# State-space rounds of a decoder kernel: block sums by accumulated transposes, a third block convolved on TensorE, ScalarE's side work placed by half units

## The reference

```python
for i in range(4):                                   # x: 8 x 100 x 256
    h = rms(x, norm_w[i])
    xi, z = split(h @ W_in[i].T)                     # 512 channels each
    xc = silu(conv_b[i] + sum(shift(xi, 3-k) * conv_w[i][:, k] for k in range(4)))
    delta, Bm, Cm = split(xc @ W_x[i].T)             # 64, 16, 16
    delta = softplus(delta @ W_dt[i].T + b_dt[i])
    A = -exp(A_log[i])                               # 512 x 16 states
    deltaA, BX = exp(delta * A), (delta * xc) * Bm
    hs = scan(deltaA, BX)                            # h_t = deltaA_t h_{t-1} + BX_t
    y = sum_n(hs * Cm) + D[i] * xc                   # over the 16 states
    x = x + (y * silu(z)) @ W_out[i].T
```

## Time and profile before

| | |
|---|---|
| median of 3 runs | 1289.17 us (1286.73 to 1289.67) |
| the profiled execution | 1286.74 us, its span 1285.0 us |
| mean granted TensorE clock | 0.949 of 2.4 GHz |
| busy over the span | PE 88%, DVE 82%, ACT 64%, POOL 60% |
| state-space rounds | from 354 to about 1056 us |

### The profile page before, as it was taken

How to read it: one execution, slowest core, us unless ns; L and a number is a source line. 1 busy time by engine, 2 the same in 40 slices (tenths; PEclk the granted TensorE clock), 3 DMA queues, 4 the chain that set the end, 5 groups by cost and what they waited for, 6 DMA issues and landing times.

```text
span 1285.0 us, 17476 instructions
## 1 busy us (share of the span) xinstructions
PE 1128.5 (88%) x5960; PEld 660.0 (51%) x5960; DVE 1050.3 (82%) x1642; ACT 825.1 (64%) x1816; POOL 775.4 (60%) x641
## 2 busy tenths in 40 slices
PE   7798888879759998998998999989989689999974
PEld 3455555544325454554554545545545346666643
DVE  4577777675689999999999999999999985676657
ACT  1455555655466786777767767877776436788763
POOL 6001111100389898998998999989989952554202
PEclk9899999998979999999998999989999899999878
DMA  7000002000510600502404107014042003100000
GB/s 211 13 13 13 13 13 73 2 1 3 201 44 0 217 34 2 205 17 88 162 1 181 42 1 251 1 54 168 1 150 88 1 11 90 34 18 18 2 1 26
DMA packets 22141, 79.13 MB, mean 62 GB/s; under 512 B 4935, under 2 KB 8847, under 8 KB 21138
## 3 DMA queue, kind: packets, MB, share of 16 engines
q1 hardware_dynamic: 22054, 78.02, 17.7%
HBM read 76.77 MB, written 1.24 MB: 61 GB/s over the span
## 4 chain that ended last, share of the span: by engine, by line
PE 42%; DVE 33%; ACT 10%; POOL 8%; issue 7%; DMA 0%; DVEq 0%; SPq 0%; POOLq 0%; ACTq 0%
PE ps L675 38%; DVE ps L2089 10%; DVE arena L2094 6%; DVE arena L2092 5%; POOL arena L2003 4%; PE ps L744 4%; ACT ps L1886 2%; DVE hstat L1213 2%; POOL arena L2015 2%; DVE arena L2052 2%; ACT L670 1%; DVE arena L1189 1%; ACT arena L936 1%; DVE arena L1179 1%; ACT arena L1776 1%
## 5 line engine op out<-in xcount | busy, mean ns | idle before, releaser
L675 PE MATMUL ps<-arena 128*32 128x100 f32 (+10 forms) x3330 | 517.4, 380 | 67.3 <-ACT arena L936 14.6
L2003 POOL TENSOR_TENSOR arena<-arena 128x1600 f32<-128x1600 f32 x128 | 456.6, 3582 | 34.0 <-DVE ps L2089 25.8
L675 PE MATMUL ps<-arena,ident 128*128 128x400 f32 x1024 | 386.5, 528 | 29.4 <-POOL arena L2015 19.9
L675 PEld LDWEIGHTS ps<-arena 128*32 128x32 f32 (+7 forms) x3330 | 259.4, 144 | 294.3 <-issue 115.9
L1886 ACT ACTIVATE ps<-arena 128x400 f32<-128x400 f32 x512 | 282.9, 589 | 184.5 <-DVE arena L2092 151.3
L2089 DVE TENSOR_TENSOR_SCAN ps<-ps,arena 128x800 f32<-128x800 f32 x176 | 320.6, 1822 | 22.8 <-ACT ps L1886 17.1
L675 PEld LDWEIGHTS ps<-arena,ident 128*128 128x128 f32 x1024 | 201.5, 200 | 196.4 <-issue 28.3
L642 POOL TENSOR_SCALAR stat<-stat 100x1 f32<-100x1 f32 (+1 forms) x44 | 8.5, 193 | 419.9 <-DVE stat L623 419.0
L2092 DVE TENSOR_TENSOR arena<-ps,arena 128x800 f32<-128x800 f32 x176 | 174.5, 991 | 6.0
L2015 POOL TENSOR_TENSOR arena<-arena 128x1600 f32<-128x1600 f32 x40 | 143.1, 3579 | 16.8 <-DVE arena L2094 16.7
L2094 DVE TENSOR_TENSOR_SCAN arena<-ps,arena 128x800 f32<-128x800 f32 x80 | 140.3, 1803 | 0.9 <-ACT ps L1886 0.7
(11 more groups left out here) (199 smaller groups left out, 1025.7 us busy)
## 6 DMA issues: line engine op xcount, KB each, us to landing
arena<-bc_scratch SPq DMA_DIRECT2D x64, 800.0 KB, 6.4
arena<-in_ctxT SPq DMA_DIRECT2D x16, 361.0 KB, 4.0
arena<-in_w_in SPq DMA_DIRECT2D x4, 1024.0 KB, 5.0
arena<-in_expT SPq DMA_DIRECT2D x1, 2048.0 KB, 12.9
arena<-in_w_out SPq DMA_DIRECT2D x4, 512.0 KB, 3.2
arena<-in_mask SPq DMA_DIRECT2D x8, 141.0 KB
arena<-in_xT SPq DMA_DIRECT2D x2, 400.0 KB, 4.1
x_tok<-in_x_tok SPq DMA_DIRECT2D x1, 800.0 KB
```

The source lines that it names most:

```text
L675: return nc.tensor.matmul(outp, lhsT, rhs, start=first, stop=last)
L2003: nc.gpsimd.tensor_tensor(bx[:, unit % BX].rearrange("p (j t) -> p j t", j=SEGMENT), bbc[:, nq].rearrange("p (j t) -> p j t", j=SEGMENT), ...
```

## The change

1. Sums by transposes (`pm_reduce`): for blocks 0 to 2 the four identity matmuls of a unit become 16 transposes of 100 columns each, accumulated in the same bank: the sum over states comes out turned (100 tokens on partitions, 4 x 128 columns). A one-row product first starts the bank. ScalarE copies a block's turned sums to SBUF (`am_turned_sums`), TensorE turns them back onto diag(D) times xc in the same bank (`pm_back`), and VectorE's y product waits for that. Block 3 is summed as before.
2. Block 1 is convolved on TensorE too: taps for three blocks, one more `pm_conv`, and on ScalarE a raw copy and an output for it; VectorE keeps block 0, three multiply-adds, one chain.
3. ScalarE's and VectorE's lists go by half units (`am_half`, `am_between`), and nearly every place in `AT` is new. The copies `am_keep` have a place of their own. On POOL the step rows of blocks 2 and 3 stand at 19 and 21 and not at 16 and 17.

```diff
-    "aK": 2,
-    "aQ": 4,
+    "aQ": 3.0,
+    "aV": 3.5,
...
-    "aV": 3,
-    "aS": 11,
...
+    "aS": 10.5,
...
-    "aD": (13, 14),
+    "aD": (13.0, 14.5),
...
-    "gD": (14, 15, 16, 17),
-    "vY": (5, 10, 13, 16),
+    "gD": (14, 15, 19, 21),
+    "aYT": (6.0, 10.0, 13.5),
+    "pY": (6, 10, 14),
+    "vY": (6.0, 10.5, 14.5, 16.5),
...
         def pm_reduce(pe, unit):
...
+            if c < CD - 1:
+                if nq == 0:
+                    mm(ps[0:S, 4 + c % 2, :], identb[0:1, 1:S + 1],
+                       identb[0:1, :].rearrange("p (o t) -> p o t", o=1).to_broadcast([1, GB, P]), True, False)
+                for j in range(SEGMENT):
+                    for b in range(GB):
+                        last = nc.tensor.matmul(ps[0:S, 4 + c % 2, b * P:(b + 1) * P],
+                                                hs[:, unit % HS, j * GT + b * S:j * GT + (b + 1) * S], ident[:, :],
+                                                is_transpose=True, start=False,
+                                                stop=nq == NQ - 1 and j == SEGMENT - 1 and b == GB - 1)
+                last.then_inc(m_red, 1)
+                return
...
+        def pm_back(pe, m, c):
+
+            pe.wait_ge(m_yt, (CD - 1) * m + c + 1)
+            pe.wait_ge(m_skip, m // G + 1)
+            o = ps[:, 4 + c % 2, 0:GT]
+            mm(o, dgd[:, c], xc[m % G][:, c], True, False)
+            for b in range(GB):
+                last = nc.tensor.matmul(o[:, b * S:(b + 1) * S], turned_rows(c)[0:S, b * P:(b + 1) * P], ident[0:S, 0:S],
+                                        is_transpose=True, start=False, stop=b == GB - 1)
+            last.then_inc(m_yb, 1)
...
+        def am_turned_sums(act, m, c):
+
+            act.wait_ge(m_red, UNITS * m + NQ * (c + 1))
+            nc.scalar.activation(turned_rows(c)[0:S, :], ps[0:S, 4 + c % 2, :], ACT.Copy).then_inc(m_yt, 1)
...
         def vm_y(dve, m, c):
...
-            dve.wait_ge(m_red, UNITS * m + NQ * (c + 1))
+            if c < CD - 1:
+                dve.wait_ge(m_yb, (CD - 1) * m + c + 1)
+            else:
+                dve.wait_ge(m_red, UNITS * m + NQ * CD)
```

More of the change, by code:

```diff
@@ L297, in decoder @@
         delta[1] = mam.take(CD, GT)
-        taps = mam.take(2, DC, P)
-        mam.at += CD * GT - 2 * DC * P
+        taps = mam.take(3, DC, P)
+        mam.at += CD * GT - 3 * DC * P
         dx = mam.take(CD, GT)
@@ L1396, in decoder @@
         m_taps = sem("m_taps")
+        m_yt, m_yb = sem("m_yt"), sem("m_yb")
         ROUNDS = G * NL
-        PREP = (["T0", "T1", "X2", "X3", "Y2", "Y3", "X0", "X1", "DB"] + [f"D{c}" for c in range(CD)]
+        PREP = (["T0", "T1", "X2", "X3", "Y2", "Y3", "X1", "X0", "Y1", "DB"] + [f"D{c}" for c in range(CD)]
                 + [f"X{e}" for e in range(CD, 2 * CD)])
@@ L1570, in pm_conv @@
             for s in range(DC):
-                last = mm(y3[:, :, s:S], taps[:, c - 2, DC - 1 - s], x3[:, :, 0:S - s], s == 0, s == DC - 1)
+                last = mm(y3[:, :, s:S], taps[:, c - 1, DC - 1 - s], x3[:, :, 0:S - s], s == 0, s == DC - 1)
             last.then_inc(m_full, 1)
@@ L1701, in mam_pe @@
                             pm_dbc(pe, m + 1)
-                        for c in range(CD):
+                        for c in (0, 1):
                             if u == AT["pD"][c]:
@@ L1831, in am_silu @@
                 return
[L1832 removed]
+            for names, c in ((("Y2", "Y3"), 2), (("X0", "Y1"), 0)):
                 for n in names:
@@ L1866, in am_skip, with am_half @@
             last.then_inc(m_skip, 1)
-        def am_unit(act, unit):
+        def am_half(act, k):
+            unit, h = divmod(k, 2)
             m, u = divmod(unit, UNITS)
@@ L1872, in am_unit @@
             l, g = divmod(m, G)
-            if nq == 0:
+            if nq == 0 and h == 0:
                 act.wait_ge(m_first, CD * m + c + 1)
@@ L1876, in am_unit @@
                     act.wait_ge(m_aneg, l + 1)
-            for h in range(2):
-                k = 2 * unit + h
-                if unit:
-                    if on_dve(unit - 1):
-                        act.wait_ge(m_cmd, dve_halves(unit - 1, h))
-                    else:
-                        act.wait_ge(m_scan, k - 1)
-                for j in range(2):
-                    n = c * NS + nq * SEGMENT + 2 * h + j
-                    last = nc.scalar.activation(psf[:, half_at(k) + j * GT:half_at(k) + (j + 1) * GT],
-                                                delta[g][:, c], ACT.Exp, scale=aneg[:, l % 2, n:n + 1])
-                last.then_inc(m_exp, 1)
+            if k >= 2:
+                before, bh = divmod(k - 2, 2)
+                if on_dve(before):
+                    act.wait_ge(m_cmd, dve_halves(before, bh))
+                else:
+                    act.wait_ge(m_scan, k - 1)
+            for j in range(2):
+                n = c * NS + nq * SEGMENT + 2 * h + j
+                last = nc.scalar.activation(psf[:, half_at(k) + j * GT:half_at(k) + (j + 1) * GT],
+                                            delta[g][:, c], ACT.Exp, scale=aneg[:, l % 2, n:n + 1])
+            last.then_inc(m_exp, 1)
         def mam_act(act):
@@ L2094, in vm_half @@
                 nc.vector.tensor_tensor_scan(y, a, bx[:, unit % BX, w], 0.0, ALU.mult, ALU.add).then_inc(m_scan, 1)
-        def vm_unit(dve, unit):
-            wait(dve, m_red, unit - HS + 1)
-            dve.wait_ge(m_bx, unit + 1)
-            for h in range(2):
-                vm_half(dve, unit, h)
         def vm_y(dve, m, c):
```

229 lines of the change are left out of this document (128 added, 101 removed).

## The result

| | before | after |
|---|---|---|
| median of the runs of one comparison | 1287.95 us (1282.80 to 1289.67, 4 runs) | 1320.06 us (1317.96 to 1322.64, 4 runs) |
| the profiled execution, its span | 1286.74, 1285.0 us | 1317.96, 1316.2 us |
| mean granted TensorE clock | 0.949 | 0.913 |

The ratio on record is 1.0271 with a 95% interval of [1.0249, 1.0293] (it is an estimate of its own; the quotient of the two medians is 1.0249): slower, as forecast (1310 us), 10 us beyond the forecast's centre.

The account below looks back on a forecast made before the run. VectorE's queue plus waits bounds a round: 84.15 - 1.5 + (1.7 + 2.4 + 1.1 + 1.4) + 0.2 + 0.9 = 90.35 us against 87.05. Six rounds +20, the first +1: 1310 us, range 1300 to 1320.

Parts of the forecast that it names:

- before 3.5: Second half of unit 3: exponentials queue behind the output rows' squares, the third waiting for output sum O1; 1.7 us a round.
- before 4.0: First half of unit 4: the gate's silu with two table loads, 4.14 us, delays the exponentials; 2.4 us a round.
- before 11.0: First half of unit 11: the convolved blocks' silu, moved to 10.5, delays the exponentials; 1.1 us a round.
- before 13.5: Second half of unit 13: first softplus, 3.69 us, moved to 13.0 where room is 2.3; wait 1.4 us a round.
- the room of two halves less two pairs: Time a ScalarE step may last between exponentials without VectorE waiting: 3.3 us between long halves, 2.3 beside one short, 1.3 between short.
- T: End of half 9.5, the second half of unit 9, from which ScalarE's steps up to exponentials 11.0 were timed.
- The transposes: TensorE's sums: 0.086 us each, 1.4 us a unit for 2.7, saving 16 us a round; cover, valued at 0.6 us.
- The clock: TensorE at 1.2 GHz after idling 22 to 31 us into the round and near 60 to 75; 0.9 us, bounds 0 to 3.2.
- Rival 2: PE stays at 1.2 GHz through the transposing blocks, making y products and reductions late: 3.2 us a round, 1325 us; chance 0.16.
- Rival 1: ScalarE enters the new places a half ahead, so only 2.3 us of wait at 4.0 is left: 1276 us; chance 0.15.
- Rival 3: Transposes run at a matmul's rate, so PE sets the round at about 95 us: 1340 us; chance 0.04.
- Rival 4: The orders cancel: two of the four waits fall away, a round of 87 us, no change; chance 0.07.

Follow-up runs that it names:

- the fourth: The changed kernel with blocks 0 and 1 both convolved on VectorE again, six steps, transposes kept: 1321.02 us, 1.0293 against the kernel before.
- the fifth experiment: The changed kernel with sums by identity matmuls and blocks 0 and 1 convolved on VectorE, only the new order left: 1322.46 us, 1.0296 against the kernel before.
- the third experiment: The changed kernel with all sums by identity matmuls again, places and block 1's convolution on TensorE kept: 1304.96 us, 1.0151 against the kernel before.
- the filled kernel: The changed kernel with nine unused 128x400 matmuls a round behind the sum of unit 3, where TensorE stood idle: 1311.34 us, 1.0210 against the kernel before.
- The first of the three kernels with other places: The changed kernel's work, transposes and third block included, with places chosen by the rule of rooms: 1271.36 us, 0.9914 against the kernel before.
- the last three kernels: Places by the rule of rooms, with transposes and third block, matmuls and third block, or the work of before: 1271.36, 1267.27, 1275.38 us.

## Why the prediction was right, point by point

| wait of VectorE, us a round | forecast | after |
|---|---|---|
| before 3.5 (third square behind O1) | 1.7 | 1.82 |
| before 4.0 (silu of z behind it) | 2.4 | 2.52 |
| before 11.0 (silu of the convolved blocks) | 1.1 | 1.63 |
| before 13.5 (softplus) | 1.4 | 1.54 |
| low clock: y product of block 0, sum of unit 15 | 0.9 | 1.92, all of it block 0 |
| what else (forecast at 15.0; found at the y product of block 3) | 0.2 | 0.27 |
| VectorE's queue without waits | 82.65 | 82.4 |
| a round | 90.35 | 92.1 |

*The bound.* Right: VectorE's queue and its waits set the round, and the room of two halves less two pairs gave all four places and, at 3.5, 4.0 and 13.5, the size within 0.15 us. The same chain, put into the kernel before, gave the same two waits.

*The convolution.* The term was right, 1.5 us off VectorE's work, but beside the transposes it bought nothing. The experiment that puts it back shows that the waits around it shrink by the same 1.5. With sums by matmuls and the same places it did take 1.5 us off a round (92.4 to 90.9).

*The wait at 11.0*, 1.63 for 1.1, and the 1.1 was partly luck: two steps of it failed, in opposite directions. The first is "Exponentials 10.0 end at T - 0.65": it leaves out the convolution between the halves 9.0 and 9.5, which by the prediction's own rule adds its 1.9 us to the room. They end at 772.22, 2.3 before T, the start of the scan 10.0. The second is "the copy of the turned sums and the result of block 1 at T + 0.55": I let the copy run at once, but it waits for TensorE:

```profile
771.11 1.11 ACT L1933 ACTIVATE ps<-arena 128x400 f32<-128x400 f32 x2 [0.61 <-DVE arena L2154]
774.56 1.80 DVE L2149 TENSOR_TENSOR_SCAN ps<-ps,arena 128x800 f32<-128x800 f32 x1
774.67 0.60 ACT L1866 ACTIVATE arena<-ps 100x512 f32<-100x512 f32 x1 [2.45 <-PE ps L1617]
```

The last sum of block 1 is ready that late. With only the first step mended, copy and result would have been done before T, exponentials 10.5 would have ended at T + 1.1, those of 11.0 at T + 6.55, and the wait would have been 0.5. That is near the 0.66 of the fourth and the fifth experiment, which convolve block 1 on VectorE. Without the copy but with the result of block 1, in the third experiment, it was still 1.2 to 1.3: there the result waits 2.61 us for TensorE.

*The transposes*, mis-sized: 0.086 us, taken from eight of 100 columns with 100 rows, against 0.11 for these at the full clock, 1.8 us a unit for 1.4. The step that failed is taking a time for 100 moving columns as one for 128: 0.086 x 1.28 is the 0.11 found. A transpose of 128 columns costs half of a matmul's 0.21 for as many. It sets no bound, since PE is busy 78.5 of 92 us, but I had expected about 70: PE gained 2 to 3.5 us and not 11. At 0.11 the twelve units save 10.8 us and not 16, and in the early stretch of low clock the work takes longer. Against the third experiment, which differs from after in the sums alone, PE is busy 5.7 us less in a round (78.6 for 84.25).

*The clock*, mis-sized: 0.9, a value chosen inside the bounds 0 to 3.2, against 1.92. The first idle place was right, 22 to 31 us into the round forecast and 24.4 to 30.7 found. The second came later than forecast: the clock is at 0.50 from 74 to 81 us into the round, for "near 60 to 75", and the 1.7 us that it might have cost at the sum of unit 15 did not come. All of the 1.92 is the y product of block 0, for which the bound was 1.5. That bound was too low because it counted only the sum of unit 4 and the turning back at 1.2 GHz. From the turning of the normalised rows to the turning back takes 7.0 us in after (748.88 to 755.87) and 4.3 in the filled kernel (749.24 to 753.50); of the 2.7 us more, 1.0 is covered (the y product there comes at 754.54), the rest is waited for. This term (1.0 more) and the one at 11.0 (0.5 more) are 9 of the 10 us between forecast and time over six rounds.

*The first and the last round.* The first was forecast at +1 and came out 0.8 us longer. The last was put at 0, "The last prepares nothing", and is 3.1 us longer. No run here isolates why. In the profiles the 4.4 us by which the stack of after begins earlier hides this, so the closeness of 30.6 to 31.2 is chance.

*Rival 2* (the low clock stays through the transposing blocks, 1325 us) is nearer in number than in kind. The clock fell once in the early part and once late, a mean of 0.91 in a round, and it was at the full level while the transposes of units 0 to 3 ran. The Trainium skill's sentence in "TensorE: Matmul & The Clock Gate", "Part 4: PE-mode transpose", that the full clock does not engage for transpose-mode is not borne out: the window 725.00 to 742.50 holds 64 of them, 0.11 us apart, at a granted clock of 1.00. One might still suspect that the matmuls ahead of them kept it up and that the transposes made it fall at 744.7. The first of the three kernels with other places speaks against that: for 15.7 us its TensorE does nothing but 104 transposes and a product of one row, with gaps of 1.4 us at most, and the clock stays at 1.00:

```profile
547.14 7.19 PE L1617 MATMUL ps<-ident,arena 128*100 128x128 f32 x64
547.14:562.88 15.74, 12.27 (x106) 11.30 (x106) 14.53 (x12) 13.66 (x35) 15.21 (x13) 1.00 0.10 35
```

What fell in after was the clock behind an idle stretch, and matmuls would have run slowly there as well: the diagonal's product at 754.41 took 0.95 us to its successor's start, against 0.67 in the filled kernel.

*Rival 1* (ScalarE carries a lead) did not come: all four waits stand in every round. *Rival 3* (transposes at a matmul's 0.21 us) did not either, 0.11 at the full clock. *Rival 4* (two waits fall away) is refuted by the 24 waits in six rounds.

What stays open: the share of the convolution's and the transposes' gain at the better places, since the last three kernels differ in places as well as in work; why the last round is longer; and how much of the 15 us between the medians of after and the third experiment lies in the rounds, of which the one profile shows 7.

## What to carry to other kernels

With two buffers between two engines that are both near full, each side step of the feeding engine has a room, the time of two buffers less two fills, and whatever exceeded it was paid in each of the middle rounds here, whatever else the change saved; write the room beside each place before moving a step, and count a step that has to wait for a third engine at that engine's time, not at its own. Work taken off the busiest engine is worth something only where that engine does not then wait: beside the transposes 1.5 us off VectorE came back as 1.5 us of waits, beside sums by matmuls it shortened the round by 1.5. And an engine made faster at one place may be slower behind it: after PE's sums took two thirds of the time, it stood idle for 6.4 us, its clock fell, and filler work of 6.2 us made the kernel 9 us faster.

## What the runs showed of the hardware

- Accumulating float32 transposes of 128 moving columns with 100 stationary columns went 0.11 us apart at the full clock (32 in 3.70 us) and 0.215 at 1.2 GHz (16 in 3.44 us); plain ones with 100 moving and 100 rows 0.086 before.
- The granted clock was 1.00 while transposes ran, also over 15.7 us with 104 of them and no other matmul than one of one row. It fell to 0.50 within an idle stretch of PE of 6.4 us and stayed there for 10.2 us; with the stretch filled with matmuls it stayed at 1.00 there, and the mean of such a round rose from 0.91 to 0.96.
- ScalarE's table loads took 1.28 us each, and the one at 736.00 began where the exponentials before it ended; a silu of 128x1600 between exponentials took 4.15 us with its two loads (736.00 to 740.15).
